# Routing by blocks, a fixed DRAM region per expert, and a shared block behind the loop: one change to a hybrid retention/FFN kernel

## The chip, the cores and the metric

The kernel runs on one core of a Trainium2 chip, in FP32 throughout. Times are device microseconds of one execution. The engines are named as the profile names them: PE (TensorE), DVE (VectorE), ACT (ScalarE), POOL (GpSimd), and SP, which only issues DMAs. They run at the same time and meet through semaphores. "PEclk" is the TensorE clock that was granted, 1.00 at 2.4 GHz and 0.50 at 1.2 GHz.

## What is computed

`x` has 2048 tokens of 128 features. A 4-layer retention block is followed by a mixture-of-experts FFN, an oscillator block, and the same FFN again:

```python
x = x + retention_4_layers(layernorm(x))
x = x + ffn(layernorm(x))
x = x + oscillator(layernorm(x))
x = x + ffn(layernorm(x))

def ffn(x):                       # 8 experts, hidden size 256
    shared_out = swiglu(x, shared_gate, shared_up, shared_down)
    logits = x @ gate_w.T
    top_id = argmax(logits)
    score = sigmoid(max(logits))
    xs = x * score[:, None]
    routed_out = sum over e of swiglu(where(top_id == e, xs, 0), r_gate[e], r_up[e], r_down[e])
    return shared_out + routed_out
```

The oscillator needs tables that depend on no token: cosines of time times frequency ("the angle") and powers of `gamma` ("the decays"), for 2048 times each.

## The kernel before

**Stages.** The program is a row of blocks, with a barrier between them: retention (0 to 351.5 us), FFN 0 (351.8 to 445.5), oscillator (446 to 533), FFN 1 (533.4 to 628.5). Inside a block each engine runs its own list of instructions in the order in which the code writes them. Nothing is reordered, so an instruction that waits holds everything written behind it on its engine. The names ending in `_ready`, `_psum` and the like are semaphores.

**FFN, front.** The tokens are 16 chunks of 128, and four chunks are a block. DVE writes the normalised chunks `xn` (L1123). PE transposes them (L1023), ACT copies the transposes out of PSUM (L969), and PE computes logits, four matmuls of 128x8 for a block (L1029). When the logits of all 16 chunks are there, DVE finds each token's expert in five instructions over all chunks (L1139 to L1146, the result is `hot`). Two matmuls (L1067, L1068) count, for each token, the tokens of its expert ahead of it. Eleven more DVE instructions (L1176 to L1191) turn the counts into `slot`, the token's row in a DRAM buffer, where the experts lie behind each other, each padded to whole tiles of 128 rows. POOL then writes the scaled tokens `xs` to these rows, one indirect DMA for each chunk (L952). The buffer has 23 tiles and was set to zero during the retention block by one DMA for each of the two FFN calls.

**Shared expert.** A block takes two matmuls of 128x512 for the gate half and two for the up half (`shared_gate`, `shared_up`, L1037; an FP32 matmul is two entries, or passes, in the trace, so a half is four), SiLU on ACT (L976), a product on DVE (`shared_hidden`, L1153), eight matmuls down (`shared_down`, L1061, 16 passes) and an addition to `x` on DVE (`shared_add`, L1159). PE writes the gate and up halves of block b+1 ahead of the down part of block b. The gate half of a block waits for the SiLU of the block before, the up half for the `shared_hidden` of the block before. Behind the fourth block PE runs three matmuls whose result nobody reads (`keep_running`, L831).

**Loop.** SP loads 23 tiles (L927) once all scatters have landed. For each tile PE transposes it (L1089), multiplies by the gate and up weights of the tile's expert (L1097) and by the down weights (L1106). ACT and DVE copy these weights to a ring (L992, L1212), addressed by the expert number that they load into a register. POOL scatters the result to the token's row (L961). SP then loads these rows in token order (`yg`, L934), and DVE adds them in four blocks (L1246); at the end of FFN 1, each block of `x` is stored behind its addition.

**Tables in FFN 0.** POOL doubles the decay table nine times ahead of its scatters (`decays`, L1822), and ACT does the last two doublings behind the first SiLU (`last_decays`, L1815, 3.60 us). DVE computes the angle (L1836) behind `xn` and ahead of the routing. `turns_rounded` and `turns_whole` follow the SiLUs of blocks 1 and 2 on ACT. `first_reduced` and the remainders (L1860) run on DVE beside the loop. `token_decays` (L1899 to L1906) follow the loop, and `sine` (L1923, L1925) on ACT.

## Time and profile before

| | us |
|---|---|
| median of 3 runs | 631.44 |
| lowest and highest | 631.32, 631.68 |
| the profiled execution's own time | 630.28 |
| its span in the trace | 628.5 |

| engine | busy us | share of the span |
|---|---|---|
| PE | 541.9 | 86% |
| DVE | 491.4 | 78% |
| ACT | 345.9 | 55% |
| POOL | 225.1 | 36% |

No engine is the bound of the whole. Retention takes 56% of the span, the two FFNs 30%. The page's slices give a first look, then one reads each stage by its timeline. A row's bracket is the idle time ahead of a group on its engine and what ended it; an arrow to "issue" means that nothing in the profile was waited for. The windows give, for a stretch, how long each engine was busy and the mean granted clock.

### The profile page before, as it was taken

What the parts mean: (1) busy time and instruction counts of PE and PEld (TensorE: products, weight loads), DVE (VectorE), ACT (ScalarE), POOL (GpSimd) and SP (SyncE); (2) the same over time, 40 slices, a digit from 0 to 9 for tenths busy, and PEclk for the clock granted to TensorE, in tenths of its full rate; (3) what the DMA queues carried; (4) which work ended last, traced back from release to release, by engine and by line L of the source; (5) the groups of instructions that cost most, each with busy time, mean ns of one, the idle gap of its engine ahead of it and who ended that gap; (6) DMA issues with size and microseconds to landing.
All of it is one profiled execution on the core that took longest, in us unless ns stands there. A gap on an engine that the chain in (4) does not pass through costs nothing. (4 is left out here: it accounts for less than half of the span.)

```text
span 628.5 us, 13515 instructions
## 1 busy us (share of the span) xinstructions
PE 541.9 (86%) x4308; PEld 415.4 (66%) x4308; DVE 491.4 (78%) x1774; ACT 345.9 (55%) x783; POOL 225.1 (36%) x234
## 2 busy tenths in 40 slices
PE   0679999999999999999976888894499996898990
PEld 0456778788788778877855555794256775655990
DVE  5979988888888888888887784778958999563552
ACT  1347878778778777777754164677044210113760
POOL 3135424424424433433410467565100000063562
PEclk9879999999999999999988779997599999699996
DMA  8916500000000000000000301232000000012225
GB/s 290 372 77 123 74 2 2 1 3 2 2 2 2 2 2 2 2 2 3 2 1 2 110 27 56 59 84 81 26 0 2 2 0 2 0 39 64 65 80 152
DMA packets 32198, 28.54 MB, mean 45 GB/s; under 512 B 4384, under 2 KB 29344, under 8 KB 31872
## 3 DMA queue, kind: packets, MB, share of 16 engines
q1 hardware_dynamic: 27232, 20.69, 12.1%
q0 software_dynamic: 2496, 5.13, 2.5%
q10 hardware_dynamic: 2400, 1.84, 0.9%
q8 instruction: 36, 0.59, 0.4%
q14 instruction: 34, 0.28, 0.1%
HBM read 18.44 MB, written 9.21 MB: 44 GB/s over the span
## 5 line engine op out<-in xcount | busy, mean ns | idle before, releaser
L442 POOL TENSOR_TENSOR att<-att,small 128x512 f32<-128x512 f32 x64 | 82.1, 1282 | 174.7 <-ACT att L345 174.7
L345 ACT ACTIVATE att<-banks 128x512 f32<-128x512 f32 x64 | 38.8, 606 | 44.9 <-PE banks L485 44.9
L961 POOL DMA_INDIRECT rows_back<-ffn_yt,ffn_xt x46 | 46.7, 1016 | 36.2 <-DVE ffn_yt L1233 35.0
L353 ACT ACTIVATE xz<-resid,nmr,rs 128x128 f32<-128x128 f32 x128 | 56.6, 501 | 5.2 <-DVE nmr L785 5.2
L485 PE MATMUL banks<-qexp,qkT 32*128 32x256 f32 x512 | 46.2, 430 | 7.7 <-DVE att L672 7.7
L672 DVE TENSOR_TENSOR att<-banks,small 128x512 f32<-128x512 f32 x64 | 44.0, 688 | 11.2 <-PE banks L485 11.0
L1097 PE MATMUL banks<-ffn_xtT,ffn_wt 128*128 128x128 f32 x368 | 49.6, 278 | 2.7 <-DVE ffn_hr L1227 1.8
L460 POOL TENSOR_TENSOR qk<-cosq,sinq 128x512 f32<-128x512 f32 x32 | 40.9, 1279 | 21.9 <-DVE cosq L721 21.8
L1097 PEld LDWEIGHTS banks<-ffn_xtT,ffn_wt 128*128 128x128 f32 x368 | 44.7, 192 | 4.1 <-ACT ffn_wt L992 2.7
L831 PE MATMUL banks<-small 128*128 128x512 f32 x38 | 24.5, 798 | 24.9 <-POOL osc_taps L1301 17.0
L952 POOL DMA_INDIRECT rows_in<-ffn_xs,ffn_slot x32 | 31.4, 980 | 31.7 <-DVE ffn_slot L1191 22.6
L501 PE MATMUL banks<-att,ve 128*32 128x128 f32 x1024 | 42.5, 285 | 0.0
L536 PEld LDWEIGHTS banks<-w,hT 128*128 128x128 f32 x256 | 33.1, 202 | 12.3 <-issue 12.2
L945 POOL MEMSET ffn_all_one<- 128x8 f32 x2 | 0.2, 105 | 113.7 <-POOLq L1293 84.6
L536 PE MATMUL banks<-w,hT 128*128 128x128 f32 x256 | 39.3, 300 | 1.8 <-ACT hT L419 1.7
L587 PE MATMUL banks<-xzT,w 128*128 128x256 f32 x128 | 37.1, 413 | 3.1 <-ACT xzT L398 3.1
L714 DVE TENSOR_TENSOR sinq<-banks,rot 128x512 f32<-128x512 f32 x32 | 22.1, 691 | 19.3 <-PE banks L596 19.1
L567 PE MATMUL banks<-small,xz 128*128 128x128 f32 x128 | 21.4, 284 | 17.0 <-ACT xz L353 17.0
L596 PE MATMUL banks<-wqkvg,xzT 128*128 128x256 f32 x128 | 34.8, 395 | 0.7 <-ACT xzT L398 0.7
L992 ACT ACTIVATE ffn_wt<-routed_sb 128x512 f32 x46 | 28.9, 630 | 10.9 <-PE banks L1106 9.0
L831 PEld LDWEIGHTS banks<-small 128*128 128x128 f32 x38 | 9.1, 255 | 35.8 <-POOL osc_taps L1301 17.2
L1037 PE MATMUL banks<-ffn_xnT,s_gu_sb 128*128 128x512 f32 x64 | 32.5, 659 | 0.0
(245 smaller groups left out, 1440.8 us busy)
## 6 DMA issues: line engine op xcount, KB each, us to landing
rot<-in_rot SPq DMA_DIRECT2D x3, 1024.0 KB, 12.4
routed_sb<-in_routed SPq DMA_DIRECT2D x1, 3072.0 KB, 11.6
rows_in<-zero_rows SPq DMA_DIRECT2D x2, 1483.5 KB, 14.4
ffn_xt<-rows_in SPq DMA_DIRECT2D x46, 64.5 KB, 1.9
ffn_yg<-rows_back SPq DMA_DIRECT2D x8, 256.0 KB, 3.9
rot<-in_rot ACTq DMA_DIRECT2D x1, 1024.0 KB, 12.3
w<-in_W SPq DMA_DIRECT2D x2, 512.0 KB, 7.6
times<-in_times SPq DMA_DIRECT2D x1, 1024.0 KB, 5.0
```

The costliest lines, as they stand in the source:

```text
L345: act.activation(att[:, c, HALF:HEADS].rearrange("p (r e) n -> p r e n", e=PER_TILE), b_att[:, 2:4, c], ACT.Copy).then_inc(s["att_raw"], 1)
L353: ins = act.activation(xz[:, n], resid[:, (g % GROUPS) * 2 + n % 2], ACT.Identity, scale=rs[:, n:n + 1], bias=nmr[:, n:n + 1])
L442: pool.tensor_tensor(att[:, c, HALF:HEADS], att[:, c, HALF:HEADS], spread(causal.unsqueeze(1), 1, HALF), ALU.mult) \
L460: pool.tensor_tensor(qk[:, v].rearrange("p a b c -> p (a b c)"), cosq[:].rearrange("p a b -> p (a b)"), sinq[:].rearrange("p a b -> p (a b ...
L485: ins = pe.matmul(b_att[:, r, c], qkT[rows, v, 1, c], qexp[rows, v % 2, c], start=True, stop=True)
L501: ins = pe.matmul(out[32 * q:32 * q + 32, :], ve[:, v, c, q, e].rearrange("p j d -> p (j d)"), att[:, c, 2 * q + e, :], start=False, stop= ...
L536: ins = pe.matmul(b_wq[:, c * P:c * P + P], hT[:, f, c * P:c * P + P], w2[:, layer(g), f, :], start=(f == 0), stop=(f == 1))
L587: ins = pe.matmul(b_xv[:, 256 * f:256 * f + 256], w1[:, layer(g), f * P:f * P + P], xzT[:, 2:4], start=True, stop=True)
L596: ins = pe.matmul(b_wq[:, 256 * c:256 * c + 256], xzT[:, c], wqkvg[:, layer(t), 0:2, :], start=True, stop=True)
L672: dve.tensor_tensor(att[:, c, 0:HALF].rearrange("p (r e) n -> p r e n", e=PER_TILE), b_att[:, 0:2, c], spread(spread(causal.unsqueeze(1).u ...
L961: pool.indirect_dma_start(rows_back, bass.IndirectOffsetOnAxis(ap=token, axis=0), yt[:, j % RING], None).then_inc(stored[j % RING], 16)
L1097: ins = pe.matmul(banks[:, 2 + v, n * P:n * P + P], wt[:, j % WT_RING, n * P:n * P + P], xtT[:, v], start=True, stop=True)
```

## The change

- **Region.** Each expert has a DRAM region of its own of 2048 rows, and there are 7 spare tiles behind them. A token's row is its expert's region start plus its rank. Slots no longer depend on how many tokens other experts have. The buffers grow from 2,944 to 17,280 rows of 129 floats each, and nine DMAs for each call set them to zero.
- **Slots by block.** `chosen`, `counted`, `scaled` and `placed` (new) do the routing for one block of four chunks. On DVE the order is `normalised(0..2)`, `chosen(0)`, `normalised(3)`, `counted(0)`, `scaled(0)`, `placed(0)`, then `chosen`, `counted`, `scaled`, `placed` of blocks 1, 2 and 3, and only then `shared_hidden(0)`. The ranks of a block take five small matmuls (10 passes); `counts` takes one more behind those of block 3. POOL's scatters of block b wait for `slot_ready` b+1.
- **Tile rows by register.** `tiles_known` (13 DVE instructions behind `shared_hidden(0)`) finds each tile's expert and its row in DRAM. SP loads this row into a register ahead of each tile load.
- **Shared block 3 behind the loop** (`LATE` = 3) on PE, ACT and DVE; its `shared_add` stands between the `yg` additions of blocks 1 and 2, and the `yg` addition of block 2 waits for it.
- **Decays in the retention block.** All eleven doublings run on POOL behind its last retention step, in a buffer shared with the rotation table `rot`. `last_decays` on ACT is gone. The angle moves behind `placed(3)`.

The core of the diff:

```diff
+                def placed(b):
+                    part = slice(BLK * b, BLK * b + BLK)
+                    rank = banks[:, 4 + b, BLK * EXPERTS:2 * BLK * EXPERTS].rearrange("p (c e) -> p c e", e=EXPERTS)
+                    dve.wait_ge(s["ranks_ready"], b + 1)
+                    link(dve.tensor_tensor(place[:, part], rank, hot[:, part], ALU.mult))
+                    link(dve.tensor_reduce(slot_f[:, part], place[:, part], AX.X, ALU.add))
+                    dve.tensor_copy(slot[:, part], slot_f[:, part]).then_inc(s["slot_ready"], 1)
...
+                for b in range(3):
+                    normalised(b)
+                chosen(0)
+                normalised(3)
+                counted(0)
                 scaled(0)
...
+                placed(0)
                 for b in range(1, NCH // BLK):
+                    chosen(b)
+                    counted(b)
                     scaled(b)
+                    placed(b)
+                if tables:
+                    tables.angle(dve)
                 shared_hidden(0)
...
+                tiles_known()
                 if tables:
                     tables.out_weights(dve)
-                for b in range(NCH // BLK):
-                    if b + 1 < NCH // BLK:
+                for b in range(LATE):
+                    if b + 1 < LATE:
                         shared_hidden(b + 1)
                     shared_add(b)
...
+                def ranks(b):
+                    out = banks[:, 4 + b, BLK * EXPERTS:2 * BLK * EXPERTS]
+                    before = route["region"]
+                    if b:
+                        pe.wait_ge(s["counted"], b)
+                        before = count[:, b - 1]
+                    pe.wait_ge(s["hot_ready"], b + 1)
+                    chunks = hot[:, BLK * b:BLK * b + BLK]
+                    pe.matmul(out, route["earlier"], chunks.rearrange("p c e -> p (c e)"), start=True, stop=False,
+                              skip_group_check=True)
+                    for c in range(BLK - 1):
+                        pe.matmul(out[:, EXPERTS * (c + 1):], route["ones"],
+                                  spread(chunks[:, c:c + 1], 1, BLK - 1 - c), start=False, stop=False,
+                                  skip_group_check=True)
+                    pe.matmul(out, route["ones"], spread(before.unsqueeze(1), 1, BLK), start=False, stop=True,
+                              skip_group_check=True).then_inc(s["ranks_ready"], 1)
...
+                        row = sp.value_load(row_of[0:1, t:t + 1], min_val=0, max_val=ROWS - P)
                         if t >= XT_RING:
                             sp.wait_ge(stored[u], stored_before(u) + (t - XT_RING) // RING * 16 + 16)
-                        sp.dma_start(xt[:, v], rows_in[call][t * P:t * P + P, :]).then_inc(x_loaded[v], 16)
+                        sp.dma_start(xt[:, v], rows_in[call][bass.ds(row, P), :]).then_inc(x_loaded[v], 16)
...
+                shared_silu(LATE)
                 if tables:
                     tables.sine(act)
...
+                shared_hidden(LATE)
+                if tables:
                     tables.token_decays(dve)
                 for b in range(NCH // BLK):
+                    if b == 2:
+                        shared_add(LATE)
+                        dve.wait_ge(s["shared_added"], LATE + 1)
...
                 run(step)(pool)
+                pool.wait_ge(s["rot_ready"], STEPS)
+                tables.decays(pool)
```

**PE at the front of FFN 1, before**, behind the transposes of the last chunks: `shared_gate(0)` and the other shared matmuls (L1037) follow the two rank matmuls (L1067, L1068). In brackets stands what a row waits for.

```order
L1029 MATMUL banks<-gate_sb,ffn_xnT 128x8 [waits ffn_xnT_ready]
...
L1067 MATMUL banks<-ffn_hot,small 128x128 [waits ffn_hot_ready]
L1068 MATMUL banks<-ffn_hot,small 128x128
L1037 MATMUL banks<-ffn_xnT,s_gu_sb 128x512 x4
L1037 MATMUL banks<-ffn_xnT,s_gu_sb 128x512 [waits ffn_gate_silu]
...
L1037 MATMUL banks<-ffn_xnT,s_gu_sb 128x512 [waits ffn_hs_ready]
...
L1061 MATMUL banks<-s_down_sb,ffn_hs 128x128 [waits ffn_hs_ready]
```

**The same place now**: the ranks of a block (L1082 to L1088), the gate and up halves of block 0 (L1065), the ranks of the next two blocks, `counts` (L1093), and then the gate half of block 1.

```order
L1082 MATMUL banks<-ffn_hot,small 128x32 [waits ffn_hot_ready,ffn_counted]
L1085 MATMUL banks<-ffn_hot,small 128x24
L1085 MATMUL banks<-ffn_hot,small 128x16
L1085 MATMUL banks<-ffn_hot,small 128x8
L1088 MATMUL banks<-ffn_count,small 128x32
L1065 MATMUL banks<-ffn_xnT,s_gu_sb 128x512 x4
L1082 MATMUL banks<-ffn_hot,small 128x32 [waits ffn_hot_ready,ffn_counted]
...
L1093 MATMUL banks<-ffn_count,small 128x8 [waits ffn_counted]
L1065 MATMUL banks<-ffn_xnT,s_gu_sb 128x512 [waits ffn_gate_silu]
...
L1065 MATMUL banks<-ffn_xnT,s_gu_sb 128x512 [waits ffn_hs_ready]
...
L1113 MATMUL banks<-s_down_sb,ffn_hs 128x128 [waits ffn_slot_ready,ffn_hs_ready]
```

The ranks of blocks 2 and 3 stand behind the eight passes of L1065, and the next gate half stands behind them.

**DVE at the front of FFN 1, before**: the slots (L1191), the scaling of the other three blocks, and `shared_hidden(0)` (L1153).

```order
L1191 CAST ffn_slot<-ffn_slot_f 128x16 [waits ffn_route_chain]
L1165 TENSOR_TENSOR ffn_xs<-ffn_xn,ffn_score 128x4x128 x3
L1153 TENSOR_TENSOR ffn_hs<-ffn_sil,banks 128x1024 [waits ffn_up_psum,ffn_gate_silu]
L1196 TENSOR_TENSOR ffn_past<-small,ffn_tiles_upto 128x184
```

**The same place now**, from the ranks of one block to those of the next, and to `shared_hidden(0)` (L1252) behind the last.

```order
L1223 TENSOR_TENSOR ffn_place<-banks,ffn_hot 128x32 [waits ffn_ranks_ready]
L1224 TENSOR_REDUCE ffn_slot_f<-ffn_place 128x4 [waits ffn_route_chain]
L1225 CAST ffn_slot<-ffn_slot_f 128x4 [waits ffn_route_chain]
L1252 TENSOR_TENSOR ffn_hs<-ffn_sil,banks 128x1024 [waits ffn_up_psum,ffn_gate_silu]
L1230 TENSOR_SCALAR ffn_ntiles<-banks 128x8 [waits ffn_ranks_ready]
```

`shared_hidden(0)` now stands behind four waits for ranks, one for each block, where one wait stood ahead of it.

**DVE at the end of FFN 1 now**: the product and the addition of the last shared block (L1252, L1258) among the additions of the gathered rows (L1328).

```order
L1252 TENSOR_TENSOR ffn_hs<-ffn_sil,banks 128x1024 [waits ffn_shared_ready,ffn_up_psum,ffn_gate_silu]
L1328 TENSOR_TENSOR xin<-xin,ffn_yg 128x512 [waits ffn_gathered0]
L1328 TENSOR_TENSOR xin<-xin,ffn_yg 128x512 [waits ffn_gathered1]
L1258 TENSOR_TENSOR xin<-xin,banks 128x512 [waits ffn_shared_ready]
L1328 TENSOR_TENSOR xin<-xin,ffn_yg 128x512 [waits ffn_gathered2,ffn_shared_added]
L1328 TENSOR_TENSOR xin<-xin,ffn_yg 128x512 [waits ffn_gathered3]
```

Before, only the four rows of L1246 stood there.

## Rows read from the trace of the kernel before

**Rows 1.** The windows: busy time of each engine and PEclk, FFN 1's routing and shared blocks.
```profile
core 0: us, PE busy (x) PEld busy (x) DVE busy (x) ACT busy (x) POOL busy (x), PEclk, DMA share, GB/s
542.80:549.50 6.70, 5.02 (x25) 4.92 (x23) 2.31 (x8) 0.81 (x2) 0.00 (x0) 0.50 0.00 0
549.60:552.90 3.30, 3.30 (x5) 1.23 (x5) 2.92 (x13) 0.00 (x0) 0.00 (x0) 0.50 0.00 0
553.10:573.00 19.90, 19.03 (x91) 12.20 (x90) 9.34 (x13) 4.99 (x6) 15.26 (x16) 1.00 0.16 51
```

**Rows 2.** Timeline of FFN 1's start; columns: start, us, engine, line, operation, idle before.
```profile
536.55 4.19 DVE L1123 TENSOR_SCALAR ffn_xn<-xin,ffn_mv,ffn_rs 128x128 f32<-128x128 f32 x16
...
540.31 1.06 PE L1029 MATMUL banks<-gate_sb,ffn_xnT 128*128 128x8 f32 x8 [0.25 <-ACT ffn_xnT L969]
...
543.18 3.42 PE L1029 MATMUL banks<-gate_sb,ffn_xnT 128*128 128x8 f32 x16
...
552.72 0.17 DVE L1191 CAST ffn_slot<-ffn_slot_f 128x16 uint32<-128x16 f32 x1
...
553.17 1.21 POOL L952 DMA_INDIRECT rows_in<-ffn_xs,ffn_slot  x1 [19.65 <-DVE ffn_slot L1191]
...
554.85 1.22 DVE L1153 TENSOR_TENSOR ffn_hs<-ffn_sil,banks 128x1024 f32<-128x1024 f32 x1 [0.16 <-PE banks L1037]
...
559.79 3.60 PE L1037 MATMUL banks<-ffn_xnT,s_gu_sb 128*128 128x512 f32 x8
...
563.23 1.95 PE L1061 MATMUL banks<-s_down_sb,ffn_hs 128*128 128x128 f32 x16
...
572.39 0.96 POOL L952 DMA_INDIRECT rows_in<-ffn_xs,ffn_slot  x1 [0.30 <-issue]
...
574.07 2.84 PE L831 MATMUL banks<-small 128*128 128x512 f32 x6 [0.78 <-DVE xin L1159]
...
576.55 0.14 PEld L1089 LDWEIGHTS banks<-small,ffn_xt 128*128 128x128 f32 x1 [0.47 <-DMA ffn_xt<-rows_in]
```

**Rows 3.** Timeline of FFN 0's start: the same places, and the angle.
```profile
359.05 2.66 DVE L1836 TENSOR_SCALAR cos_tab<-times,freqs_sb 128x2048 f32<-128x2048 f32 x2
...
368.10 0.18 DVE L1191 CAST ffn_slot<-ffn_slot_f 128x16 uint32<-128x16 f32 x1
...
370.38 1.22 DVE L1153 TENSOR_TENSOR ffn_hs<-ffn_sil,banks 128x1024 f32<-128x1024 f32 x1 [0.30 <-PE banks L1037]
...
390.05 2.84 PE L831 MATMUL banks<-small 128*128 128x512 f32 x6 [0.78 <-DVE xin L1159]
```

**Rows 4.** Timeline of FFN 0's end.
```profile
432.11 3.10 DVE L1860 SCALAR_TENSOR_TENSOR cos_tab<-turns,cos_tab 128x256 f32<-128x256 f32 x9
...
437.01 1.74 DVE L1906 RECIPROCAL out_dec<-out_dec 128x256 f32<-128x256 f32 x1
...
439.40 0.69 DVE L1246 TENSOR_TENSOR xin<-xin,ffn_yg 128x512 f32<-128x512 f32 x1 [0.64 <-DMA ffn_yg<-rows_back]
```

**Rows 5.** Timeline of FFN 1's end: the last two additions.
```profile
624.12 1.52 DVE L1246 TENSOR_TENSOR xin<-xin,ffn_yg 128x512 f32<-128x512 f32 x2 [0.85 <-DMA ffn_yg<-rows_back]
```

**Rows 6.** Timeline of FFN 1's loop: a weight copy behind a register load, and the loop's end.
```profile
574.84 0.29 DVE L1212 COPY ffn_wt<-routed_sb 128x256 f32 x1 [0.47 <-issue]
...
613.69 0.71 PE L1106 MATMUL banks<-ffn_wt,ffn_hr 128*128 128x128 f32 x4 [0.24 <-DVE ffn_yt L1233]
```

**Rows 7.** Timeline, retention's end and FFN 0: POOL and DVE at the same time.
```profile
317.05 1.26 POOL L442 TENSOR_TENSOR att<-att,small 128x512 f32<-128x512 f32 x1 [4.49 <-ACT att L345]
...
317.11 1.24 DVE L172 SCALAR_TENSOR_TENSOR vt<-vt 128x20 f32<-128x20 f32 x1
...
363.64 1.82 POOL L1822 TENSOR_SCALAR dec_tab<-dec_tab,gam_sb 128x256 f32<-128x256 f32 x2
...
363.80 0.85 DVE L1165 TENSOR_TENSOR ffn_xs<-ffn_xn,ffn_score 128x512 f32<-128x512 f32 x1
```

**Rows 8.** The page's DMA issues: the zeroing; KB each, us to landing.
```profile
rows_in<-zero_rows SPq DMA_DIRECT2D x2, 1483.5 KB, 14.4
```

272 lines of the change are left out of this document (151 added, 121 removed).

## The prediction, made before the changed kernel was run

> **What bounds the kernel now.** I read the windows first [rows 1]. From 553.1 to 573.0 PE is busy for 19.03 of 19.90 us: FFN 1 waits for PE's shared blocks, not for POOL's scatters (15.26 us busy). From 542.8 to 552.9 the granted clock is 0.50, so the routing runs on a PE at half speed. The timeline [rows 2] shows the chain. The expert choice needs all logits (end 546.60), `slot` is written at 552.72, the first scatter starts at 553.17 and the last ends at 573.35. In the same time PE works through four shared blocks, `keep_running` starts at 574.07, and the first tile is transposed from 576.55, where the row names the tile load as the last thing waited for. So two chains end within a microsecond: slots, scatters, tile load; and `shared_hidden(0)`, shared blocks, `keep_running`. Taking time from one alone gives almost nothing. FFN 0 has the same shape [rows 3]. From there to 613.69 the loop makes 26 steps, 1.43 us each [rows 2, 6].
>
> **Prices.** A short pass (logits) costs 1.06/8 = 0.13 us at clock 1.00 and 3.42/16 = 0.21 at 0.50 [rows 2]. Four passes of 512 columns cost 1.80 at 1.00 (3.60/8 each) and I take 3.4 at 0.50. Thirteen DVE instructions of 8 to 128 elements fill 3.30 us, 0.25 each with gaps [rows 1]; the new ones have 4 to 32 elements, nearer the CAST's 0.17 [rows 2], so I take 0.22. `chosen` (5) is 1.1, `counted` (2) 0.44, `scaled` 0.2 + 0.7, `placed` (3) 0.7, `ranks` (10 passes) 1.3 or 2.1.
>
> **Front of FFN 1, walked in order.** The 12 chunks of `xn` written first take 3.2 of the 4.19 us. Logits of block 0 end at 541.3 as now; `chosen(0)` ends 542.4. PE is then in logits(1), and ranks(0) runs 542.6 to 544.6 at the half clock. `placed(0)` ends 545.3, and POOL starts at 545.5 instead of 553.17, 7.7 earlier. That is the gain. On PE follow transposes(3) and logits(2), (3), to 548.8, and ranks(1), to 550.9; `placed(1)` ends 551.5. Then come gate(0), to 554.3, and up(0), to 557.3 (the clock rises in it, as it does at 553 now). Only then does ranks(2) run, to 558.5, though `hot` of block 2 is ready at about 552.8: DVE waits 5.7 us for eight passes that it doesn't need. `placed(2)` and `chosen(3)` take until 560.3, ranks(3) until 562.4, `placed(3)` until 563.0, and `shared_hidden(0)`, behind it on DVE, ends at 564.3. It ends at 556.1 now [rows 2]: **8.2 late**. PE has only gate(1) to do in this wait, and that stands behind ranks(3) and `counts` too.
> From `shared_hidden(0)` to the loop are 20.5 us now: three blocks of 5.2 us (the step from 559.79, with 3.60 and 1.95 us of work in it) and 4.9 for the last down part, addition and `keep_running` (2.84). After the change two blocks are left, 15.3, and gate(1) at the half clock adds 1.7: 17.0. The loop starts at 581.3 instead of 576.7: 8.2 - 5.2 + 1.7 = 4.7, and **+4.6** before rounding. The scatters are done at 569.0 (the slots of block 3 hold the last four), 4 us ahead of 573.35 and 12 ahead of need. The early slots buy nothing, since the other chain is the later one. `tiles_known` (13 instructions, 3 us of DVE) lies behind `shared_hidden(0)`, while PE computes up(1) and gate(2), and is hidden.
>
> **Front of FFN 0.** The same walk starts POOL at 362.8, 5.8 earlier than the slots of 368.10 allow, and ends `placed(3)` at 378.7. The angle (2.66) is now behind that and ahead of `shared_hidden(0)`, which ends at 382.6 instead of 371.6, 11.0 late [rows 3]. One block fewer and a higher clock at the end give 5.0 back: `keep_running` ends at 398.9 instead of 392.9, **+6.0**. The walk, laid over the kernel before, meets its trace within 0.5 us (first scatter, `keep_running`). What it can't know is the granted clock: with the higher clock kept in most of the stretch it gives +2.7 and +0.4. I book **+5.2** for FFN 0 and **+4.6** for FFN 1.
>
> **End of FFN 0.** Behind the loop DVE has the remainders (3.10 from 432.11), then `token_decays` to 438.75, and waits 0.64 for the gathered rows before the first addition at 439.40 [rows 4]. `shared_hidden(3)` puts 1.22 and a short wait for SiLU between them: `token_decays` ends 1.5 later, at about 440.3, 0.9 past the landing. `shared_add(3)` adds 0.7 between additions that follow each other. **+1.6**. The sine on ACT starts later by the SiLU (1.0) and a wait for PE's gate half, and ends some 4 us later than 439.05, at 443.4, ahead of the block's end at 445.5: hidden, and worth the excess if the loop's end shifts by 2 more.
> **End of FFN 1.** DVE waits 0.85 for the third gather [rows 5], and `shared_add(3)` (0.69) fits there, if PE has the block done: gate, SiLU, product and down take some 7 us from 614.4, to 621.5, ahead of 624.1. **0**, at most 0.7.
>
> **Rows by register.** SP loads a number ahead of each DMA. DVE's own load of this kind leaves 0.47 idle [rows 6], far below the loop's 1.43, and later loads run ahead of PE. Only the first is on the path: 0 to 0.5, taken as 0.3 for each call, **+0.6**. Its wait for `tiles_known` is over long before.
>
> **Decays and zeroing.** POOL is idle behind its last retention step until the barrier at 351.8. By the two steps of 256 elements in 1.82 us, doubling the size each time, eleven doublings take some 18.6 us, and end near 341, before the barrier. What DVE may lose: one row shows a 20-element DVE instruction taking 1.24 instead of 0.18 beside a POOL tensor_tensor, another DVE instruction took 0.85 beside the very POOL operation that moves here, against 0.69 [rows 7]. I take **+0.2**, from 0 up to 5. The Trainium skill (page "SBUF — State Buffer", section "SBUF: two separate sides") says that DVE and POOL take one port pair in turn, for whole instructions, when DVE reads two SBUF inputs. The first pair of rows agrees; in the second, 0.16 was lost where the rule asks for most of 0.9. By the rule alone every two-input DVE instruction of the last steps would wait, which is rival D below. In return `last_decays` (3.60 on ACT) and POOL's doublings leave FFN 0. They give nothing: POOL's last one ends at 365.46 [rows 7], ahead of the slots of 368.10, and ACT's lie beside PE's work. The zeroing DMAs move 17.8 MB instead of 2.97. At the 1483.5 KB in 14.4 us of [rows 8] that is 173 us at most, in the background of a retention whose engines wait for no DMA then and which lasts to 351: 0. Smaller tables at the start: **-0.1**.
>
> **Sum.** 5.2 + 4.6 + 1.6 + 0.6 + 0.2 - 0.1 = +12.1. On the profiled execution's own 630.28 this makes 642.4; the median of the runs lies 1.16 above that execution, so the forecast is **643.5**.
>
> **Rivals.**
> A, the forecast: DVE's wait for ranks behind up(0) makes the shared chain late. Chance 0.56, 639 to 648.
> B, the same, but the higher clock is held in the routing. FFN 0 costs 2.7 and FFN 1 0.4, with the same 2.3 of the rest 636.8: 633 to 638. For it: the new order puts matmuls where PE stood idle. Against: they are short ones, and the clock was 0.50 with PE busy 5.02 of 6.70 us [rows 1]. Chance 0.15.
> C, faster. With clock 1.00 in the whole front, each ranks costs 1.3 and each half 1.8, so up(0) ends about 6 us sooner, and `shared_hidden(0)` ends at 555.7, no later than now. Then the block taken out counts in full: -5.7 in FFN 1 and -0.3 in FFN 0, with +2.3 of the rest: 627.7. It turns on `shared_hidden(0)` of FFN 1 ending less than 5 us late. Chance 0.13.
> D, POOL's doublings hold DVE in the retention's end. By the first pair of [rows 7] a held instruction loses 1.06 us. The instructions of POOL that are at least as long as the one there (1.26) are about five, each holds one: +5, 648.5. Against it speaks the second pair. Chance 0.08.
> E, the register loads pace the loop. This needs more than 1.43 us for a load and a DMA issue; at 1.6 it costs 0.17 x 23 x 2 = 8 more. 651. Chance 0.03.
> F, the change in the two chains cancels: within 0.2%, 630.2 to 632.7, which is about what a measurement can tell from no change. Chance 0.05.
>
> **How the numbers follow.** The predicted time is A's. The range must leave out no more than 2 in 10. It goes from 630.5, which holds B and F and leaves C out, to 649, which holds A and D. Faster: C, 0.13. Same: F, 0.05. Slower: A, B, D and E, 0.82.
>
> **What would show it.** Right: in the windows of FFN 1 a PE idle for some 5 us before gate(1), `shared_hidden(0)` ending near 564 and 382, the first scatters near 545.5 and 363, `keep_running` still the last before the loop, the tile loads landed long before. Wrong: PEclk at 1.00 through the routing (B or C), DVE instructions above 0.3 us beside L1900's doublings before 351 (D), steps of the loop above 1.43 (E), or `shared_hidden(0)` no later than now, which would take away the ground of the forecast.

## The result, and the profile after

| | before | after |
|---|---|---|
| median of 4 runs, us | 631.56 | 642.18 |
| lowest to highest | 631.32 to 631.95 | 637.87 to 643.37 |
| span of the profiled execution | 628.5 | 641.6 |

The changed kernel is slower by the ratio 1.0165, 95% interval 1.0132 to 1.0198. The forecast was 643.5, from 630.5 to 649. The times after spread over 5.5 us, where the four of before lie within 0.6; thirteen more runs of the kernel before, beside the first experiments, spread over 8.2 (626.15 to 634.31), so the spread is not the change's own. In the table of the experiments the ratios leave out slow runs (over 1.5% above the fastest of the same kernel) and the medians do not: without them the kernel before at 657.64 has 656.05, hidden_again has 650.51, and grouped, one of whose four runs took 1327.81, has 644.36.

Where the 13.1 us between the two spans are, stage by stage (the rows add up to 12.9 before rounding; the rest lies behind the last addition). "Front" is the time from the start of an FFN (POOL's first memset) to the transpose of its first tile, "loop" from there to the last copy of a result tile, "end" from there to the next block or, in FFN 1, to the last addition.

| stage | before | after | difference | forecast |
|---|---|---|---|---|
| retention | 351.8 | 354.1 | +2.3 | +0.1 |
| FFN 0, front | 41.0 | 46.2 | +5.2 | +5.2 |
| FFN 0, loop | 39.5 | 38.5 | -0.9 | +0.3 |
| FFN 0, end | 13.6 | 14.9 | +1.3 | +1.6 |
| oscillator | 87.7 | 87.5 | -0.2 | 0 |
| FFN 1, front | 43.3 | 48.2 | +4.8 | +4.6 |
| FFN 1, loop | 38.0 | 38.1 | +0.1 | +0.3 |
| FFN 1, end | 10.9 | 11.0 | +0.1 | 0 |

The front of FFN 1 in the timeline of the kernel after (start, us, engine, line, operation, idle before); L840 is `keep_running`, L1065 the gate and up halves, L1082 the first matmul of a block's ranks:

```profile
541.23 0.10 POOL L961 MEMSET ffn_all_one<- 128x8 f32 x1 [84.42 <-POOLq L1374]
...
554.00 1.03 POOL L966 DMA_INDIRECT rows_in<-ffn_xs,ffn_slot  x1 [12.67 <-DVE ffn_slot L1225]
...
558.65 6.39 PE L1065 MATMUL banks<-ffn_xnT,s_gu_sb 128*128 128x512 f32 x8
...
564.88 0.30 PE L1082 MATMUL banks<-ffn_hot,small 128*128 128x32 f32 x2
...
566.11 0.19 DVE L1223 TENSOR_TENSOR ffn_place<-banks,ffn_hot 128x32 f32<-128x32 f32 x1 [4.26 <-PE banks L1088]
...
567.86 0.61 PE L1082 MATMUL banks<-ffn_hot,small 128*128 128x32 f32 x2 [1.78 <-DVE ffn_hot L1201]
...
570.41 5.63 PE L1065 MATMUL banks<-ffn_xnT,s_gu_sb 128*128 128x512 f32 x8
...
570.74 1.22 DVE L1252 TENSOR_TENSOR ffn_hs<-ffn_sil,banks 128x1024 f32<-128x1024 f32 x1
...
575.83 0.96 POOL L966 DMA_INDIRECT rows_in<-ffn_xs,ffn_slot  x1 [0.30 <-issue]
...
578.86 5.83 SPq L943 DMA_DIRECT2D ffn_xt<-rows_in  x6
...
586.73 2.84 PE L840 MATMUL banks<-small 128*128 128x512 f32 x6 [0.78 <-DVE xin L1258]
```

Set it beside [rows 2]. The block begins 7.8 us later (541.23 against 533.4), and POOL's first scatter only 0.8 later (554.00 against 553.17): relative to the block it starts 7.0 us earlier. The last scatter ends at 576.79, 35.6 us into the block instead of 39.9. Nobody uses this: the tile loads are issued at 578.86, and PE comes to the first tile only at 589.4. PE does the eight passes of gate(0) and up(0) from 558.65 to 565.04; the row at 566.11 shows DVE idle for 4.26 us until the ranks behind them are there; PE in its turn is idle for 1.78 at 567.86, waiting for the next choice; and `shared_hidden(0)` ends at 571.96, 30.7 us into the block instead of 22.7 [rows 2]. The first tile waits until `keep_running` is done (its last row ends at 589.57).

The windows of the same stretch (busy time and count of each engine, PEclk, DMA share, GB/s):

```profile
core 0: us, PE busy (x) PEld busy (x) DVE busy (x) ACT busy (x) POOL busy (x), PEclk, DMA share, GB/s
547.10:550.40 3.30, 3.05 (x28) 2.81 (x26) 1.60 (x8) 1.89 (x4) 0.00 (x0) 1.00 0.00 0
550.50:564.10 13.60, 13.60 (x47) 10.50 (x47) 7.35 (x32) 0.90 (x3) 7.60 (x8) 0.50 0.12 36
564.20:567.50 3.30, 1.87 (x12) 1.28 (x11) 1.21 (x7) 0.65 (x2) 0.82 (x2) 1.00 0.07 21
567.60:574.30 6.70, 6.44 (x17) 4.41 (x18) 5.09 (x20) 0.46 (x2) 5.14 (x6) 0.50 0.15 49
574.40:586.70 12.30, 10.67 (x60) 7.50 (x58) 5.06 (x8) 2.90 (x4) 1.92 (x2) 1.00 0.20 52
```

The lower clock covers 550.5 to 564.1 and again 567.6 to 574.3, 20.3 us in all. Before, it covered 542.8 to 552.9 behind the first logits [rows 1].

FFN 0 and the retention's end in the kernel after; L1912 is the angle, L1898 the doubling, L164, L174 and L763 instructions of the retention's normalisation:

```profile
337.22 5.66 POOL L1898 TENSOR_SCALAR shared_tab<-shared_tab,gam_sb 128x1024 f32<-128x1024 f32 x2 [0.17 <-POOL shared_tab L1898]
...
337.33 1.03 DVE L164 TENSOR_TENSOR vt<-vt,vv 128x20 f32<-128x20 f32 x1
...
338.82 0.18 DVE L174 TENSOR_TENSOR vt<-vt,vv 128x20 f32<-128x20 f32 x1
...
342.13 0.78 DVE L763 TENSOR_SCALAR vv<-mv 128x20 f32<-128x20 f32 x1
...
354.10 0.10 POOL L961 MEMSET ffn_all_one<- 128x8 f32 x1 [11.22 <-POOLq L301]
...
366.56 1.19 POOL L966 DMA_INDIRECT rows_in<-ffn_xs,ffn_slot  x1 [12.36 <-DVE ffn_slot L1225]
...
379.27 2.75 DVE L1912 TENSOR_SCALAR shared_tab<-times,freqs_sb 128x2048 f32<-128x2048 f32 x2
...
382.05 1.22 DVE L1252 TENSOR_TENSOR ffn_hs<-ffn_sil,banks 128x1024 f32<-128x1024 f32 x1
...
383.32 3.60 PE L1065 MATMUL banks<-ffn_xnT,s_gu_sb 128*128 128x512 f32 x4 [1.30 <-DVE ffn_hs L1252]
...
397.61 2.84 PE L840 MATMUL banks<-small 128*128 128x512 f32 x6 [0.43 <-DVE xin L1258]
```

The DVE instruction at 337.33 took 1.03 us and that at 342.13 took 0.78, where their kind takes 0.18 and 0.16 a few rows on: both lie beside POOL's doubling of 1024 elements. In FFN 0 `shared_hidden(0)` ends at 383.27, 29.2 us into the block (before 19.8, [rows 3]), and PE's up(1) waited 1.30 for it.

The end of FFN 0 and of FFN 1 (L1981 ends `token_decays`, L1258 is `shared_add`, L1328 the addition of the gathered rows):

```profile
442.01 1.22 DVE L1252 TENSOR_TENSOR ffn_hs<-ffn_sil,banks 128x1024 f32<-128x1024 f32 x1 [0.19 <-issue]
...
445.04 1.75 DVE L1981 RECIPROCAL out_dec<-out_dec 128x256 f32<-128x256 f32 x1
...
446.70 0.63 DVE L1328 TENSOR_TENSOR xin<-xin,ffn_yg 128x512 f32<-128x512 f32 x1
...
449.65 0.67 DVE L1258 TENSOR_TENSOR xin<-xin,banks 128x512 f32<-128x512 f32 x1
...
636.04 0.68 DVE L1258 TENSOR_TENSOR xin<-xin,banks 128x512 f32<-128x512 f32 x1
...
637.23 1.29 DVE L1328 TENSOR_TENSOR xin<-xin,ffn_yg 128x512 f32<-128x512 f32 x2 [0.52 <-DMA ffn_yg<-rows_back]
```

The first three rows answer to [rows 4] and the last to [rows 5]. In FFN 0 the wait of 0.64 ahead of the first addition is gone, and everything behind it is later by what the block costs. In FFN 1 the addition of the late block took the place of a wait: 0.52 of idle is left of 0.85.

### The profile page after: what moved, and what is told of

Read it like the earlier page. It is cut to its first block and busy times, and to the rows that moved or that the text cites. A ratio compares the mean times of both kernels' runs of the same rounds, so it can differ in the third digit from the quotient of the medians.

```text
span 641.6 us, 14047 instructions
## 1 busy us (share of the span) xinstructions
PE 563.3 (88%) x4384; PEld 430.7 (67%) x4384; DVE 503.4 (78%) x1846; ACT 342.7 (53%) x785; POOL 228.9 (36%) x238
## 5 line engine op out<-in xcount | busy, mean ns | idle before, releaser
L975 POOL DMA_INDIRECT rows_back<-ffn_yt,ffn_xt x46 | 46.8, 1018 | 56.9 <-DVE ffn_yt L1310 55.1
L494 PE MATMUL banks<-qexp,qkT 32*128 32x256 f32 x512 | 46.8, 435 | 5.9 <-DVE att L681 5.9
L966 POOL DMA_INDIRECT rows_in<-ffn_xs,ffn_slot x32 | 33.0, 1032 | 36.7 <-DVE ffn_slot L1225 28.2
L840 PE MATMUL banks<-small 128*128 128x512 f32 x38 | 25.4, 822 | 19.1 <-POOL osc_taps L1382 11.5
L545 PEld LDWEIGHTS banks<-w,hT 128*128 128x128 f32 x256 | 32.9, 201 | 12.6 <-issue 12.5
L596 PE MATMUL banks<-xzT,w 128*128 128x256 f32 x128 | 37.7, 419 | 3.1 <-ACT xzT L405 3.1
L1065 PE MATMUL banks<-ffn_xnT,s_gu_sb 128*128 128x512 f32 x64 | 38.7, 759 | 1.4 <-DVE ffn_hs L1252 1.3
L576 PE MATMUL banks<-small,xz 128*128 128x128 f32 x128 | 21.6, 285 | 18.9 <-ACT xz L360 18.9
L723 DVE TENSOR_TENSOR sinq<-banks,shared_tab 128x512 f32<-128x512 f32 x32 | 22.1, 691 | 19.4 <-PE banks L605 19.2
L494 PEld LDWEIGHTS banks<-qexp,qkT 32*128 32x128 f32 x512 | 20.5, 187 | 16.3 <-issue 13.1
## 6 DMA issues: line engine op xcount, KB each, us to landing
rows_in<-zero_rows SPq DMA_DIRECT2D x16, 1032.0 KB, 18.5
shared_tab<-in_rot ACTq DMA_DIRECT2D x1, 1024.0 KB, 11.8
```

Of the source, the lines that this page charges most:

```text
L494: ins = pe.matmul(b_att[:, r, c], qkT[rows, v, 1, c], qexp[rows, v % 2, c], start=True, stop=True)
L545: ins = pe.matmul(b_wq[:, c * P:c * P + P], hT[:, f, c * P:c * P + P], w2[:, layer(g), f, :], start=(f == 0), stop=(f == 1))
L596: ins = pe.matmul(b_xv[:, 256 * f:256 * f + 256], w1[:, layer(g), f * P:f * P + P], xzT[:, 2:4], start=True, stop=True)
L975: pool.indirect_dma_start(rows_back, bass.IndirectOffsetOnAxis(ap=token, axis=0), yt[:, j % RING], None).then_inc(stored[j % RING], 16)
L1065: ins = pe.matmul(banks[:, n, :], w["s_gu"][:, n], rhs, start=True, stop=True)
```

## The experiments

Each kernel was timed beside the kernel before on the same chip, in three groups of runs. The group matters here. In the first (the first four rows) the kernel before takes 631.45 us, as it did beside the changed kernel (631.56), which is why these four are set beside 642.18. In the second (the next four) it took 654.60 and in the third (the last four) 657.64: every kernel is longer there, by different amounts (section on the hardware). So times are compared within a group. The record gives chip 6 for the first two groups and chip 15 for the third. What makes the groups differ is therefore not known, and where an expectation below says "first chip" and "second chip", read first and second group.

| kernel | this | before, same group | ratio, 95% interval | fronts of FFN 0, FFN 1 |
|---|---|---|---|---|
| four_ahead | 647.84 | 631.45 | 1.0295, 1.0221 to 1.0368 | 49.0, 48.7 |
| hidden_first | 634.91 | 631.45 | 1.0059, 1.0023 to 1.0094 | 42.7, 39.9 |
| decays_in_ffn | 639.71 | 631.45 | 1.0137, 1.0072 to 1.0201 | 43.8, 48.1 |
| filled | 639.80 | 631.45 | 1.0137, 1.0075 to 1.0200 | 47.0, 43.3 |
| split_decays | 642.78 | 654.60 | 0.9834, 0.9771 to 0.9896 | 44.1, 43.7 |
| grouped | 645.09 | 654.60 | 0.9850, 0.9774 to 0.9926 | 42.8, 46.9 |
| grouped_split | 641.28 | 654.60 | 0.9791, 0.9733 to 0.9850 | 42.7, 46.8 |
| before_late | 652.01 | 654.60 | 0.9968, 0.9928 to 1.0008 | 48.2, 44.4 |
| after_again | 653.98 | 657.64 | 0.9973, 0.9934 to 1.0012 | 47.5, 48.1 |
| hidden_again | 650.53 | 657.64 | 0.9878, 0.9814 to 0.9942 | 46.2, 47.8 |
| grouped_again | 644.04 | 657.64 | 0.9817, 0.9761 to 0.9873 | 41.0, 43.8 |
| grouped_split_again | 640.91 | 657.64 | 0.9775, 0.9720 to 0.9829 | 41.6, 46.7 |

The fronts are those of the one profiled execution of each kernel, to be set beside 41.0 and 43.3 (before) and 46.2 and 48.2 (after).

**The order of DVE's work** (hidden_first). My theory was that `shared_hidden(0)` is late because it stands behind four waits for ranks.

```diff
                 placed(0)
-                for b in range(1, NCH // BLK):
+                chosen(1)
+                counted(1)
+                scaled(1)
+                placed(1)
+                for b in (2, 3):
                     chosen(b)
                     counted(b)
                     scaled(b)
-                    placed(b)
+                shared_hidden(0)
+                placed(2)
+                placed(3)
                 if tables:
                     tables.angle(dve)
-                shared_hidden(0)
```

> DVE's order alone: chosen, counted and scaled of blocks 2 and 3 come first, then shared_hidden(0), and only then placed(2), placed(3) and, in FFN 0, the angle. No work is added or taken away, PE's order is as changed. Theory (the order makes the shared chain late): in FFN 1 shared_hidden(0) ends some 5 us sooner (26 instead of 30.7 us after the block's start), PE's idle 1.8 us ahead of ranks(3) goes, and in FFN 0 so does the 1.3 us ahead of up(1) with part of the angle's 2.7: -3 to -4, 638 to 639. Rival (PE is short of time, by the 38 passes of ranks added and by the lower clock, not by waiting): shared_hidden(0) is sooner, and the loop starts less than 1.5 us sooner in the two fronts together, 641 or more.

It took 634.91 (ten runs, 631.43 to 637.68), 7.3 less than the changed kernel's 642.18 (637.87 to 643.37), twice what I expected, with the same instructions on every engine. The front of FFN 1, in its timeline and windows:

```profile
562.70 0.30 PE L1082 MATMUL banks<-ffn_hot,small 128*128 128x32 f32 x2
...
562.97 1.22 DVE L1252 TENSOR_TENSOR ffn_hs<-ffn_sil,banks 128x1024 f32<-128x1024 f32 x1 [0.15 <-PE banks L1065]
...
563.74 0.39 PE L1082 MATMUL banks<-ffn_hot,small 128*128 128x32 f32 x2
...
565.05 0.19 DVE L1223 TENSOR_TENSOR ffn_place<-banks,ffn_hot 128x32 f32<-128x32 f32 x1 [0.33 <-PE banks L1088]
...
565.08 3.68 PE L1065 MATMUL banks<-ffn_xnT,s_gu_sb 128*128 128x512 f32 x8
...
579.43 2.84 PE L840 MATMUL banks<-small 128*128 128x512 f32 x6 [0.78 <-DVE xin L1258]
```

```profile
547.70:554.40 6.70, 6.45 (x59) 6.21 (x57) 4.96 (x23) 2.69 (x6) 0.00 (x0) 1.00 0.01 2
554.50:561.20 6.70, 6.35 (x17) 4.05 (x17) 5.08 (x22) 0.67 (x3) 5.33 (x5) 0.50 0.13 41
561.30:579.00 17.70, 16.48 (x90) 11.47 (x88) 10.58 (x30) 3.74 (x5) 10.58 (x11) 1.00 0.16 49
```

The ranks of blocks 2 and 3 now run back to back behind up(0) (562.70, 563.74), since both choices were made while PE did the eight passes. DVE waits 0.33 instead of 4.26, PE's idle 1.78 is gone, and `shared_hidden(0)` ends 21.9 us into the block instead of 30.7. The lower clock covers 6.7 us of the stretch instead of 20.3; from 561.3 on it was 1.00. gate(1) and up(1), 5.63 us after the change, take 3.68. The whole front in one window, of the changed kernel and of hidden_first:

```profile
541.23:589.40 48.17, 44.44 (x174) 30.57 (x175) 26.95 (x112) 6.99 (x13) 15.78 (x17) 0.73 0.12 34
```

```profile
542.25:582.12 39.87, 37.58 (x175) 25.28 (x176) 27.10 (x112) 7.20 (x13) 16.08 (x17) 0.85 0.11 34
```

The front is 8.3 us shorter. PE is idle for 3.7 us in the one and 2.3 in the other, so only 1.4 of it is idle time; 6.9 us are the same matmuls at a mean clock of 0.85 instead of 0.73. That is the part I had not counted.

But not all of the 8.3 is the order's. PE's list is the same in both kernels and DVE's differs only behind `scaled(2)`, so nothing ahead of the end of up(0) can come from the edit. These are the times from the start of the block, in us, FFN 0 and FFN 1, of the profiled executions:

| kernel | up(0) ends | `shared_hidden(0)` ends | first tile |
|---|---|---|---|
| before | 18.5, 21.3 | 19.8, 22.7 | 41.0, 43.3 |
| the changed kernel | 20.5, 23.8 | 29.2, 30.7 | 46.2, 48.2 |
| hidden_first | 19.4, 20.6 | 21.6, 21.9 | 42.7, 39.9 |
| four_ahead | 19.3, 20.6 | 28.1, 26.5 | 49.0, 48.7 |
| filled | 22.8, 20.4 | 31.3, 26.3 | 47.0, 43.3 |
| after_again | 19.7, 20.6 | 30.5, 27.0 | 47.5, 48.1 |
| hidden_again | 19.7, 24.0 | 21.5, 25.3 | 46.2, 47.8 |

In FFN 1 up(0) already ends 3.2 us sooner in hidden_first. There the clock was 1.00 for 6.8 us from 547.6 where the changed kernel had it for 3.4 from 547.1. The changed kernel's own second profile (after_again) has up(0) at 20.6 too: this part is the luck of one execution. The order's part lies behind it. From up(0) to `shared_hidden(0)` 6.9 us became 1.3 in FFN 1 and 8.7 became 2.2 in FFN 0; up to the first tile that is worth 5.1 and 2.3. The whole kernel gained less than the two fronts' 11.8 us, because in this execution FFN 0 also begins 2.3 later (356.41) and its loop takes 2.7 longer (41.2), where the edit changes nothing.

In FFN 0 DVE does the angle and `tiles_known` ahead of `shared_hidden(1)`, and PE waits for it:

```profile
384.73 0.18 DVE L1245 TENSOR_SCALAR ffn_row_of<-ffn_row_f 128x23 int32<-128x23 f32 x1
...
386.20 1.22 DVE L1252 TENSOR_TENSOR ffn_hs<-ffn_sil,banks 128x1024 f32<-128x1024 f32 x1
...
387.47 3.53 PE L1065 MATMUL banks<-ffn_xnT,s_gu_sb 128*128 128x512 f32 x4 [2.31 <-DVE ffn_hs L1252]
```

PE stood idle for 2.31 us ahead of up(2). So the order is a cause, and of those tried the largest; and in FFN 0 the same effect is left one block on.

**The clock** (filled). The rival that I had given 0.15 and 0.13 says that the clock in the routing decides.

```diff
                 transposes(2)
+                keep_running(pe, banks[:, 3, :], small, 1)
                 logits(1)
+                keep_running(pe, banks[:, 3, :], small, 1)
                 ranks(0)
...
                 logits(3)
+                keep_running(pe, banks[:, 3, :], small, 2)
                 ranks(1)
```

> Four more matmuls of 128x512 whose result nobody reads, in each front: one ahead of logits(1), one ahead of ranks(0), two ahead of ranks(1). They cost 4 x 0.86 = 3.4 us of PE at clock 1.00. Theory of the clock (the lower clock in the front of FFN 1, 0.50 from 550.5 to 564.1, is what the short matmuls bring): PEclk stays at 1.00 in the routing, gate(0) and up(0) take 3.6 instead of 6.4, ranks 1.3 instead of 2.1, and the two fronts come out 2 to 5 us shorter together: 637 to 640. Rival (the order alone makes the chain late, the clock follows from waits that remain): PEclk stays as it was or falls a little later, and the kernel gets slower by 3 to 6, 645 to 648.

It took 639.80, 2.4 less than the changed kernel, though it does more; the runs of the two overlap (638.47 to 641.39, and 637.87 to 643.37), so the difference is not clear of the noise. The windows of its FFN 1:

```profile
549.00:569.40 20.40, 18.30 (x110) 13.64 (x109) 13.36 (x57) 3.90 (x9) 9.78 (x10) 1.00 0.10 31
569.50:584.00 14.50, 13.12 (x62) 8.41 (x60) 7.38 (x19) 3.08 (x4) 5.85 (x7) 0.88 0.18 50
```

The clock is 1.00 from 549.0 to 569.4, where the changed kernel had 0.50 for 20.3 us. gate(0) and up(0) take 3.68 us instead of 6.39. The front of FFN 1 is 43.3, 4.8 less, with the dummy matmuls in it. The front of FFN 0 is 0.8 longer; there the clock fell later, and the angle keeps `shared_hidden(0)` back anyway. Against the profiled execution of the changed kernel the clock is thus worth some 8 us of FFN 1's front (an estimate: 4.8, and the 3.4 spent). Part of that would have come in another execution without any dummy: `shared_hidden(0)` ends at 26.3 here, and at 26.5 in four_ahead, whose list ahead of it is the changed kernel's. The order's wait is still there, 5.9 us from up(0) to `shared_hidden(0)`. So the clock and the order are two causes that act on the same stretch; how much of the low clock the order's waits bring was not separated.

**The block behind the loop** (four_ahead).

```diff
-        LATE = NCH // BLK - 1
+        LATE = NCH // BLK
...
-                shared_silu(LATE)
...
-                shared_hidden(LATE)
...
-                    if b == 2:
-                        shared_add(LATE)
-                        dve.wait_ge(s["shared_added"], LATE + 1)
```

> The changed kernel with all four shared blocks ahead of the loop again (block 3 is no longer behind it); all else as changed. If the start of the loop is set by PE's shared blocks, as the prediction says, the block costs 5.2 us in each front, and the ends of the FFNs give back 1.3 and 0.1 (the additions of FFN 0's end came 1.3 late relative to the loop): +9, about 651 by the median of 642.2. Rival: the scatters or the tile loads set the loop's start, and the block taken out was hidden; then the kernel gets no more than 1 us slower, or 1.4 faster by the ends.

It took 647.84, 5.7 more than the changed kernel. So the block was on the path, and the rival (hidden) falls. The two fronts grew by 2.8 and 0.6 in the profiled execution, not by 5.2 each, while the end of FFN 0 gave back 1.3 as expected. But in that execution the clock was 1.00 from 549.1 to 555.9 and from 562.7 to 569.6, and `shared_hidden(0)`, which stands ahead of all that the edit changes, ended 1.1 and 4.2 us sooner than in the profiled execution of the changed kernel. From there to the first tile the block costs 3.9 and 4.8 (20.9 against 17.0, and 22.2 against 17.5), near the 5.2 of the forecast.

**The decays** (decays_in_ffn, split_decays). The first puts them back in FFN 0 as before the change; the second, on hidden_first, leaves nine doublings in the retention's end and gives the two longest to ACT in FFN 0.

```diff
-                pool.wait_ge(s["rot_ready"], STEPS)
-                tables.decays(pool)
...
                 pool.memset(all_one[:], 1.0).then_inc(s["ones_set"], 1)
+                if tables:
+                    tables.decays(pool)
...
+                        if b == 0:
+                            tables.last_decays(act)
```

> The decays back in FFN 0: nine doublings on POOL ahead of its scatters and the last two on ACT behind the first SiLU, none in the retention block; all else as changed. Theory (POOL's long doublings hold DVE in the retention's end): the start of FFN 0 comes 1.6 us sooner, of the 2.34 it is late, and POOL starts its scatters 1.5 later, which the shared chain hides: -1.6, 640.6. Rival (the retention is late by the zeroing DMAs or by the clock): no change, 642.2.

> The kernel hidden_first (634.9) with the decays split: nine doublings on POOL in the retention's end, the last two, which took POOL 3.17 and 5.67 us, on ACT behind the first SiLU of FFN 0 as before the change. Theory (POOL's longest doublings hold DVE: two DVE instructions of the retention's end took 0.6 to 0.9 longer beside the one of 5.67): no DVE instruction above 0.5 us between 320 and 350 apart from those that take it anyway, the tail of the retention some 1 us shorter, -1: 634. Rival (the later start of FFN 0 is the phase of the lower clock in the tail, 342 to 359, and the spread of the start): no change.

decays_in_ffn took 639.71, 2.5 less, with runs (638.17 to 640.77) that overlap those of the changed kernel; FFN 0 begins 1.2 sooner (352.92), where I expected 1.6. Take as the tail the time from the start of the retention's last but one `att` multiplication on POOL (317.05 in [rows 7]) to the start of FFN 0: 34.7 before and 36.4 after. In the eight profiled executions with all eleven doublings there it is 36.4 to 37.7, mean 36.8. In the three with none there it is 34.7, 36.0 and 36.1; with nine, 32.9, 33.9 and 36.1. Between 325 and 351 split_decays shows no DVE instruction that lost more than 0.25 us. So the longest doublings seem to cost about 1 us or 2, but the tail of one kind differs by as much from one execution to the next, and the price is not measured more closely. The direct loss in the changed kernel is the two rows shown, 0.85 and 0.62. split_decays has no neighbour of its own kind (hidden_first) in its group, so its time alone says nothing; grouped_split lies 3.1 us below grouped in both groups (the run of 1327.81 left out), with the same edit between them, where 1 was expected.

**The short passes** (grouped). On hidden_first, the routing in two groups: chunks 0 to 3, then 4 to 15. The edit does more than save passes: ranks of chunks 4 to 7 no longer stand ahead of gate(0), and in FFN 0 the angle stands behind `shared_hidden(0)`.

```diff
-                    for c in range(BLK - 1):
-                        pe.matmul(out[:, EXPERTS * (c + 1):], route["ones"],
-                                  spread(chunks[:, c:c + 1], 1, BLK - 1 - c), start=False, stop=False,
-                                  skip_group_check=True)
+                    chunks = hot[:, :, GROUPS[g]]
+                    pe.matmul(total, route["ones"], chunks, start=True, stop=True)
+                    pe.matmul(within, route["earlier"], chunks, start=True, stop=False)
...
                 shared_gate(0)
+                ranks(1)
                 shared_up(0)
-                ranks(2)
-                ranks(3)
                 counts()
```

> On hidden_first (634.9), the routing in two groups instead of four blocks: chunks 0 to 3, then 4 to 15. Each group takes three matmuls (6 passes) and a scan on DVE, so the passes for ranks and counts fall from 42 to 14 in each FFN. PE writes gate(0) ahead of the ranks of the second group and up(0) behind them. Theory (PE's added short passes are what is left of the lateness): 28 passes fewer at 0.13 to 0.21 us, 3.6 to 5.9 us in each front less what PE idles for the second group, so -3 to -7 together: 628 to 632. Rival (waits and the clock set the front, not the passes): less than 2 us in both fronts together, 633 or more. The floor is the scatters' chain: they end 33 to 34 us after an FFN's start and the first tile is there 3 us later, 37, against the loop's 42.7 and 39.9.

> The kernel grouped with the decays split as in split_decays. If the two edits add up: 1 us below grouped, 627 to 631. If ACT's last_decays (3.6 us behind the first SiLU of FFN 0) now lies on the path, since the front is shorter, FFN 0 gives the 1 us back.

Both ran in the second group, and hidden_first in the first, so they were run again beside it and beside the changed kernel:

> The changed kernel once more, beside the mended ones on one chip. The four kernels of the last call ran where the kernel before took 654.6 instead of 631.5. If this chip is like the first: 642, 10.6 above the kernel before. If it is like the second, all are longer, and only their order tells something: by the theory (the lateness comes of the order of DVE and PE) this one stays the slowest of the four.

> hidden_first once more (shared_hidden(0) ahead of placed(2) and placed(3), nothing else changed). On a chip like the first 7 below the changed kernel, 635. Rival (the 7 us were the luck of the clock's phase in one call): within 2 us of the changed kernel.

> The kernel grouped (routing in two groups, 14 short passes for ranks and counts instead of 42), now beside hidden_first. Theory (the added passes hold PE): 3 to 7 us below hidden_first, 628 to 632. Rival (the passes lie in waits): within 2 us of hidden_first.

> The kernel grouped_split (two groups, and the last two decay doublings on ACT in FFN 0), which was 13 below the kernel before on the second chip. On a chip like the first: 1 us below grouped, 627 to 631, that is 0 to 4 below the kernel before at 631.5. Rival (its gain was the second chip's alone): above 631.5.

The order of the four is as the theories said: 653.98, 650.53, 644.04, 640.91. The sizes are not. hidden_again lies 3.5 below the changed kernel, half of the 7 expected, with runs that overlap (644.31 to 654.56, and 650.28 to 657.57). The last two rows of the table above say what happened: behind up(0) the order saves 1.4 and 3.6 us up to the first tile, and `shared_hidden(0)` follows up(0) after 1.8 and 1.3 us instead of 10.8 and 6.3; but in its profiled FFN 1 up(0) itself came 3.3 us later. So the effect of the order is there again, some 5 us in the two fronts with this group's late signals in it, and the 7.3 between the first medians is not confirmed as its size.

grouped lies 6.5 below hidden_first in the third group. Its up(0) ends 18.4 us into both blocks, against 19.7 and 24.0. That is what fewer passes ahead of up(0) should do, but the edit moves other work too, so the passes' own share is not shown. The changed kernel is no slower than the kernel before there (0.9973, interval 0.9934 to 1.0012), and grouped_split is faster than the kernel before, by 1.5 to 2.8% over the two groups. What the last does where the kernel before takes 631.5 was not run; that stays open, and with it whether any of these beats the kernel before there. The best one run there, hidden_first, does not (1.0059).

**One part alone** (before_late). The kernel before, with the shared block 3 behind the loop and nothing else.

```diff
-                for b in range(NCH // BLK):
-                    if b + 1 < NCH // BLK:
+                for b in range(LATE):
+                    if b + 1 < LATE:
                         shared_gate(b + 1)
...
                 run(step)(pe)
+                pe.wait_ge(s["xtT_ready"], TILES)
+                shared_gate(LATE)
+                pe.wait_ge(s["hr_ready"], TILES)
+                shared_up(LATE)
+                shared_down(LATE)
```

> The kernel before with one part alone: the shared block 3 behind the loop. Theory of the prediction (two chains end within a microsecond ahead of the loop, and the scatters with the tile load are one of them): the front gains no more than 0.5 us in each call, the end of FFN 0 costs 1.4, so +0.5 to +1.4, 632 to 633. Rival (PE's shared blocks alone set the loop's start): -5.2 in each front, +1.4 at the end, 622.5.

It took 652.01 against 654.60, between 4.7 faster and 0.5 slower. The 9 us of the rival are excluded; my +0.5 to +1.4 lies at the edge of the interval or outside. Nor does the time show the two chains that end together, since this group has waits of its own, as its FFN 0 shows:

```profile
378.51 3.60 PE L1042 MATMUL banks<-ffn_xnT,s_gu_sb 128*128 128x512 f32 x8
...
381.94 1.95 PE L1066 MATMUL banks<-s_down_sb,ffn_hs 128*128 128x128 f32 x16
...
384.25 1.22 DVE L1163 TENSOR_TENSOR ffn_hs<-ffn_sil,banks 128x1024 f32<-128x1024 f32 x1 [3.65 <-remote]
...
394.14 0.69 DVE L1169 TENSOR_TENSOR xin<-xin,banks 128x512 f32<-128x512 f32 x1 [8.66 <-remote]
...
394.97 3.75 PE L1066 MATMUL banks<-s_down_sb,ffn_hs 128*128 128x128 f32 x16 [11.08 <-DVE xin L1169]
```

Its tile loads do say something. They are issued 38.9 and 38.2 us into the two blocks, and a load takes 1.9 us on the page of the kernel before. By this estimate the first tile could not have come before 40.8 and 40.1, even with PE's signals in time; the kernel before has 41.0 and 43.3. So the scatters' chain leaves next to nothing to gain in FFN 0, as the theory has it, and some 3 us in this execution of FFN 1.

## Why the prediction was right, point by point

- **The ground of the forecast held.** "DVE waits 5.7 us for eight passes that it doesn't need": it waited 4.26 for ranks(2), of which 1.2 are the ranks themselves, and PE 1.78 for the choice behind it. hidden_first takes this wait away and the lateness with it. `shared_hidden(0)` was forecast 8.2 late in FFN 1 and is 8.1 late; 11.0 in FFN 0, and is 9.3. The fronts were booked at +5.2 and +4.6 and measure +5.2 and +4.8. One sign did not show: PE was to be idle for some 5 us ahead of gate(1), and was idle for 1.78 there.
- **The closeness in FFN 1 is partly luck.** The 8.1 holds for an execution whose clock fell early in the routing. The same list, in four_ahead and after_again, has `shared_hidden(0)` 3.9 and 4.3 late, under the 5 that rival C named. The profiled execution was the slowest of the four, and in the third group the changed kernel is not slower at all. The forecast was right for the group in which it was tested.
- **The early slots bought nothing**, as said: the last scatter of FFN 1 ends 4.3 us earlier in the block, and the tile loads are issued 10.5 us before the first tile is transposed.
- **The terms behind it.** From `shared_hidden(0)` to the first tile the change was to give back 3.5 in FFN 1 (5.2 for the block, less 1.7 for gate(1) at the half clock), and gives 3.2; in FFN 0 5.0, and gives 4.1. So in FFN 0 both terms were too large by 1 to 2 us and partly cancelled, and +5.2, booked for the clock instead of the +6.0 of the walk, was right by luck as much as by reason. What the order costs was under-sized in the expectation of hidden_first: 5.1 and 2.3 us behind up(0), where I expected 3 to 4 for both, because I counted PE's waits and not the clock behind them.
- **The retention was mis-sized:** +0.1 forecast, +2.3 measured. Of these 1.65 lie in the tail (36.36 against 34.71). Two DVE instructions were held for 1.5 us together, and the clock went to 0.50 for 17.1 us from 342.3 instead of 13.7 from 341.4. This is the sign that I had named for rival D, at 1.5 us instead of 5. The rule on the port pair of VectorE and GpSimd (the Trainium skill, "SBUF — State Buffer", section "SBUF: two separate sides"), which I weighed for D, asks that a DVE instruction with two SBUF inputs wait for the whole GpSimd instruction. The rows do not bear that out: the held L164 was done at 338.36 and POOL's doubling at 340.06, and inside the same doubling L174 (`vt` and `vv`, two inputs too) began at 338.82 and took its usual 0.18. Why these two were held is open. The other 0.7 was there by the third `att` multiplication, at 44 us. before_late, whose retention is that of the kernel before, was later at that point too (44.8) and had a tail of 36.0, so much of the +2.3 may be no more than a spread between executions.
- **The loops** were booked at +0.6 for the register loads and came to -0.8 together. The first load is off the path, as the chain is PE's. The same loop took 41.2 us in FFN 0 of hidden_first, so a us either way is its own spread.
- **The ends**: +1.6 and 0 forecast, +1.3 and +0.1 measured.
- **The zeroing** cost nothing. From 100 to 300 us PE is busy for all of it, as it was before, with a third of the DMA time taken (the zeroing ends near 152 us). The third `att` multiplication of the retention is 0.7 us later than before and the last but one, at 317.75, is still 0.7 later, so nothing was lost in between:

```profile
100.00:300.00 200.00, 200.00 (x2016) 159.16 (x2015) 173.17 (x689) 153.20 (x384) 78.60 (x63) 1.00 0.33 49
```

The sum of the stages was forecast at +12.1 and the spans differ by 13.1; the medians differ by 10.6, as the profiled execution of the changed kernel lies 1.2 above its median and that of the kernel before 1.3 below.

## What to carry to other kernels

An instruction's place in an in-order queue is part of its price: work that another engine needs must not stand behind a wait for that engine's own next task, so make all choices first, then release the long operation, then place. Two executions of one list can differ by some 3 us through the clock alone, so compare two kernels from the point where their lists part, and only then count idle time and clock. Making one of two chains earlier that end together is worth little until the other is shortened as well; here that was read from the rows and not shown by a run. A margin of 2% must be tested in more than one group of runs.

## What the runs showed of the hardware

**PE's signals came late in two of the three groups.** In the second and third, where the kernel before took 654.6 and 657.6 us, rows appear whose idle time ends with "remote": the semaphore rose, and no instruction on record had just ended. The profiles of the four kernels of the first group, of the kernel before and of the changed kernel have no such row; the eight of the other groups all have some. In before_late above, the down part is on record as ended at 383.89, and the addition that waits for it began at 394.14. In hidden_again:

```profile
379.67 1.95 PE L1113 MATMUL banks<-s_down_sb,ffn_hs 128*128 128x128 f32 x16
...
379.72 0.19 DVE L1223 TENSOR_TENSOR ffn_place<-banks,ffn_hot 128x32 f32<-128x32 f32 x1 [3.31 <-remote]
...
382.58 1.02 ACT L1002 ACTIVATE ffn_sil<-banks 128x1024 f32<-128x1024 f32 x1 [8.09 <-remote]
```

ACT was idle for 8.09 us, though the gate half that it waited for is on record as ended 4.6 us before (377.98). The retention shows nothing of it: its last but one `att` multiplication starts at 316.8 to 318.7 us in the six profiles without such rows and at 317.1 to 318.8 in the eight with them. All "remote" rows lie in the FFNs. The loops are longer there too: 43.6 and 41.8 us for the changed kernel, where the first execution took 38.5 and 38.1. PEclk shows little of it: the mean over the runs of the kernel before is 0.941, 0.931 and 0.928 in the three groups. The chip's number does not explain it, since the first two groups have the same. Since the ends of matmuls are modelled in these records, the likeliest reading is that PE worked slower than its records say; it was argued, not tested.

**The clock of one stretch differs with order, with filling and from one execution to the next.** The front of FFN 1 had the clock at 0.50 for 20.3 us behind its first 6 in the changed kernel and for 6.7 in hidden_first; the changed kernel's second profile (after_again) had it for 13.6. Four dummy matmuls of 128x512 kept it at 1.00 for 20.4 us, where no profile without them kept it for more than 6.8 in that routing. In the changed kernel it stayed at 0.50 for 13.6 us (550.5 to 564.1) with PE busy for all of them, first with passes of 8 to 128 columns and then with passes of 512.
